# A two-layer language tower on one core: the expert stage with 71 blocks of 256 rows instead of 72

## The chip, the cores and the metric

The kernel runs on one core of one Trainium2 chip. The metric is the device time of the whole program in microseconds (us); lower is better. The program is one launch: every stage below runs once, one after the other, on the core's five engines (PE does the matmuls, DVE and ACT work on vectors, POOL gathers, scatters and computes a few small values, SP does nothing but issue DMAs) and its 16 DMA engines.

## The reference, cut to what matters

64 x 128 tokens with 192 features pass through an embedding with a layer norm, an attention layer, a mixture-of-experts layer, a second attention layer and a tree-shaped feed-forward layer. All of it is float32. The expert layer is the one that the change is about:

```
logits = xf @ Wr + br                       # xf: 8192 tokens x 192
gates = jax.nn.softmax(logits, axis=-1)
top_g, top_i = jax.lax.top_k(gates, K)      # K = 2 of E = 8 experts
for e in range(E):
    w_e = jnp.sum(top_g * (top_i == e), axis=-1)
    h = jax.nn.gelu(xf @ W1[e] + b1[e], approximate=False)   # 192 -> 768
    y = h @ W2[e] + b2[e]                                     # 768 -> 192
    out = out + w_e[:, None] * y
```

Each token counts for two experts alone, so 16384 rows have to be computed, in groups by expert.

## The kernel before, in words

The tokens are held in 64 tiles of 128 rows. The program has five stages.

**Layer 0** (embedding, first attention, router logits) is a software pipeline over the 64 tiles. `pipeline` (line 98) writes one step per tile on each engine; in step n a stage of age a works on tile n - a. It writes 12 steps out (for this layer), loops over the rest four steps at a time, and writes the steps that drain the pipeline out behind the loop. All engines have the same step order, and semaphores couple them. On SP (line 763), step n issues, in this order: two DMAs of 64 rows each that fill `posb`, the position rows of tile n (line 770); one DMA that writes zero rows from the tile `zrow` to a 64th of `xs_d` (line 773); and two DMAs of 64 rows that store the finished rows of tile n - 8 to `h1_d` (line 780). `posb` has two buffers, so the DMAs for tile n wait until DVE has read those of tile n - 2 (`emb_rd`). DVE reads `posb` and the gathered word rows `tok` in its `emb` step (line 635), one step after the load in the schedule. All of SP's DMAs stand on one queue, which the profile calls q1. POOL gathers `tok` on queue q0.

**Why zeros:** `xs_d` is the input of the expert stage in DRAM, `NBLK` blocks of 256 rows. The rows of an expert begin at a multiple of 256 and the blocks are not all full, so all rows are zeroed first. The view used at line 759 cuts `xs_d` into 64 pieces (one per tile), each of p partitions with `ZROWS` rows of 192 values behind each other. With 72 blocks there are 72 * 256 / 64 = 288 rows in a piece: 96 partitions of 3 rows.

**Routing** places each (token, choice) pair at a row of `xs_d`; then POOL scatters the normalised rows there (line 987), after it has waited for all 64 zero-fill DMAs (`xs_zero`, line 981). DVE also works out `etabi`, the expert of each block (lines 954 to 957); blocks behind the last group get expert 7 and hold zeros.

**The expert stage** is a pipeline over `NBLK` blocks with ages load 0, h 1, y 2. Each block loads its 256 rows, the weights of its expert (`w1h` and `w2h`, through a register that SP reads from `etabi`), splits the first weight into two parts on DVE, does 54 matmuls (line 1106 has 30 of them per block, line 1081 24), 6 gelu activations on ACT, and stores 256 rows to `ys_d`. `pipeline` writes 8 blocks out, loops over the other 64 in 16 rounds of 4, and drains with 2 steps.

**Layer 1** gathers the two expert rows of each token from `ys_d` and runs the second attention; **the last stage** does the tree-shaped layer and writes the output.

At the start of the program ACT too issues DMAs, on a queue of its own, q10 (lines 814 to 824): four loads of 21 rows (`wout`), four loads of 128 rows (`wqk`, `wv`, `wo`, `win`), three loads of 65 rows (`wqk`, `wv`, `wo`), one of 64 rows (`win`), and two stores to `rel_d` of 128 x 12 = 1536 rows each. ACT issues no other DMA in the whole program.

The functions that the change touches follow.

Of the kernel before, what the change touches and what calls it, by code (L numbers as in the profile page):

```python
# [15 lines left out]
T, B = 64, 128  # L16
# [6 lines left out]
E, TOPK, I = 8, 2, 768  # L23
NI = I // 128
BLK = 256
NBLK = T * B * TOPK // BLK + E
REL = 33
MAXREL = 16
LPAD = B - 1 - MAXREL
# [31 lines left out]
def upto(t, tiles=NT):  # L61

    return max(0, min(t + 1, tiles)) if isinstance(t, int) else t + 1


def after(eng, sem, value):

    if not isinstance(value, int) or value > 0:
        eng.wait_ge(sem, value)


UNROLL = 4
# [25 lines left out]
def pipeline(eng, ages, body, links=None, per=0, tiles=NT):  # L98


    head = UNROLL * (2 if max(ages.values()) < 8 else 3)

    for n in range(head):
        body(Step(ages, n, n // 2, n % UNROLL, tiles))
    at0 = links.at if links else 0
    with eng.Fori(0, (tiles - head) // UNROLL) as i:
        if links:
            links.base, links.at = at0 + i * (per * UNROLL), 0
        for p in range(UNROLL):
            body(Step(ages, UNROLL * i + (head + p), 2 * i + (head + p) // 2, p, tiles))  # L110
    if links:
        assert links.at == per * UNROLL, (links.at, per)
        links.base, links.at = 0, at0 + per * (tiles - head)
    for n in range(tiles, tiles + max(ages.values())):
        body(Step(ages, n, n // 2, n % UNROLL, tiles))


# [4 lines left out]
def settle(eng, spare):  # L122

    eng.sem_inc(spare, 1)


def tower(nc, ids_h, typ_h, tok_w, pos_w, type_w, gamma, beta,
          wqk0, wv0, wo0, w1h, b1h, w2h, b2h, wr, wqk1, wv1, wo1, relblk, rel32, win, wout, out):
    h1_d = nc.dram_tensor("h1_d", [T * B, D], F32).ap()
    xs_d = nc.dram_tensor("xs_d", [NBLK * BLK, D], F32).ap()  # L130
    ys_d = nc.dram_tensor("ys_d", [NBLK * BLK, D], F32).ap()
    route_d = nc.dram_tensor("route_d", [2 * TOPK, T * B], F32).ap()
    rel_d = [nc.dram_tensor(f"rel_d{p}", [B, ROWW], F32).ap() for p in range(2)]

    with ExitStack() as ctx:
        def sb(name, shape, dt=F32):
            return ctx.enter_context(nc.sbuf_tensor(name, shape, dt))
# [4 lines left out]
        def sem(name):  # L142
            return ctx.enter_context(nc.semaphore(name))
# [109 lines left out]
        small = sb("small", [128, 12, NT])  # L253
        etab = sb("etab", [128, NBLK])
        etabi = sb("etabi", [128, NBLK], I32)
        cnt = sb("cnt", [128, 6, E])
        cnti = sb("cnti", [128, E], I32)
        etmp = probT[0][:, 0:NBLK * E].rearrange("p (j e) -> p j e", e=E)
        wout4 = sb("wout4", [128, 4, D])


        def dsem(name):
            return sem("ld_" + name)

        const_ld = dsem("const")
        N_CONST = 14
        ZROWS = 3
        ids_ld = dsem("ids")
        late_ld = dsem("late")
        pool_c = sem("pool_c")  # L270
# [18 lines left out]
        def pool_steps(pool, l):  # L289
# [15 lines left out]
            def body(st):  # L305
# [16 lines left out]
                if st.has("z"):  # L322
                    rsqrt(st.tile("z"), st.two("z"), "mvz_ok", mvz, "rsz_ok", rsz, vepsz)
            pipeline(pool, ages, body, ch, 3 - l)

        def pe_transpose(pe, dst, src):
# [8 lines left out]
        def pe_steps(pe, l):  # L335
# [5 lines left out]
            def body(st):  # L341
# [166 lines left out]
                if st.has("z"):  # L508
                    pe.wait_ge(S["zn_ok"], done("z"))
                    pe_transpose(pe, ps_t[:, 256:512], zn[st.two("z")][:]).then_inc(S["zT_ps"], 1)  # L510
            pipeline(pe, ages, body)

        def act_steps(act, l):
# [5 lines left out]
            def body(st):  # L519
# [87 lines left out]
                if st.has("z"):  # L607
                    b = st.two("z")
                    act.wait_ge(S["zT_ps"], done("z"))
                    act.activation(zT0[b][:], ps_t[:, 256:384], ACT.Copy)  # L610
                    act.activation(zT1[b][0:D1, :], ps_t[0:D1, 384:512], ACT.Copy).then_inc(S["zT_sb"], 1)
            pipeline(act, ages, body)

        def dve_steps(dve, l):
# [131 lines left out]
        def _(sp):  # L746
# [11 lines left out]

            zr = xs_d.rearrange("(n p r) d -> n p (r d)", n=NT, r=ZROWS)
            sp.wait_ge(zero_ok, 2)  # L760
            h1_v = h1_d.rearrange("(t n c) d -> n c t d", n=NT, c=2)

            def body(st):
                if st.has("gather"):
# [4 lines left out]
                    for c in range(2):  # L769
                        sp.dma_start(posb[b][64 * c:64 * c + 64, :],  # L770
                                     pos_w[bass.ds(2 * t + c, 1), :].to_broadcast([64, D])).then_inc(M_["pos"][b], 16)

                    sp.dma_start(zr[bass.ds(t, 1)].rearrange("o p d -> (o p) d"), zrow[0:zr.shape[1], 0:ZROWS * D])\
                        .then_inc(xs_zero, 16)
# [90 lines left out]
        with nc.Block() as block:  # L865
# [9 lines left out]
            def _(pool):  # L875

                pool.iota(etabi[:], pattern=[[BLK, NBLK]], base=0, channel_multiplier=0).then_inc(B_["pool"], 1)
                pool.iota(cnti[:], pattern=[[-1, E]], base=E, channel_multiplier=0).then_inc(B_["pool"], 1)
# [118 lines left out]
        y_st = [sem(f"y_st{p}") for p in range(2)]  # L997
# [18 lines left out]
        with nc.Block() as block:  # L1016
            @block.sync
            def _(sp):
                hv = h1_d.rearrange("(t b) d -> b t d", b=B)

                def body(st):
                    before2 = upto(st.n - 2, NBLK)
                    if isinstance(st.n, int) and 4 <= st.n < 8:


                        c = st.n - 4
                        sp.dma_start(hres[:, 16 * c:16 * c + 16, :], hv[:, 16 * c:16 * c + 16, :])\
                            .then_inc(h1_ld[c], 16)
                    if st.has("load"):
                        t, b = st.tile("load"), st.two("load")  # L1030
                        ex = sp.value_load(etabi[0:1, bass.ds(t, 1)], min_val=0, max_val=E - 1)

                        after(sp, D_["h_sb"], NH * before2)
                        settle(sp, spare)
                        rows_ = xs_d[bass.ds(t * BLK, BLK), :].rearrange("(s p) d -> p s d", s=2)
                        sp.dma_start(xs[b][:, :, 0:D], rows_).then_inc(w1_ld[b], 16)
                        sp.dma_start(xs[b][:, :, D:XW], rows_[:, :, 128:D]).then_inc(w1_ld[b], 16)
                        loads = [(w1[b][0], w1h[bass.ds(ex, 1), 0:128, :]), (b1s[b][:], b1h[bass.ds(ex, 1)])]
                        loads += [(w1[b][1][r:r + D1, :], w1h[bass.ds(ex, 1), 128:, :]) for r in (0, D1)]
                        for dst, src in loads:  # L1040
                            sp.dma_start(dst, src.rearrange("o k i -> (o k) i")).then_inc(w1_ld[b], 16)

                        after(sp, D_["y_sb"], before2)
                        settle(sp, spare)
                        sp.dma_start(probT[b][:, 0:NI * D], w2h[bass.ds(ex, 1), :, :].rearrange("o k i -> (o k) i"))\
                            .then_inc(w2_ld[b], 16)
                        sp.dma_start(b2s[b], b2h[bass.ds(ex, 1), :].to_broadcast([128, D])).then_inc(w2_ld[b], 16)
                    if st.has("y"):
                        t, b = st.tile("y"), st.two("y")
                        sp.wait_ge(D_["y_sb"], upto(t, NBLK))  # L1050
                        settle(sp, spare)
                        sp.dma_start(ys_d[bass.ds(t * BLK, BLK), :].rearrange("(s p) d -> p s d", s=2), ys[b][:])\
                            .then_inc(y_st[b], 16)
                pipeline(sp, ages_d, body, tiles=NBLK)
                for p in range(2):
                    sp.wait_ge(y_st[p], 16 * (NBLK // 2))

            @block.tensor
            def _(pe):
# [335 lines left out]
def build(nc, arrays):  # L1395
    args = [nc.dram_tensor(n, x.shape, mybir.dt.from_np(x.dtype), kind="ExternalInput").ap()
            for n, x in arrays.items()]
    out = nc.dram_tensor("out_0_dram", [T, B, D], F32, kind="ExternalOutput").ap()
    tower(nc, *args, out)
# [11 lines left out]
```

## Time and profile before

| | |
|---|---|
| median of three runs | 2311.49 us (2299.59 to 2316.12) |
| the profiled execution's own time | 2312.43 us |
| its span, first to last instruction | 2310.7 us |
| PE busy | 1958.2 us, 85% of the span |
| DVE busy | 1397.8 us, 60% |
| ACT busy | 1011.0 us, 44% |
| POOL busy | 578.5 us, 25% |
| layer 0 | from 0 to about 640 us |
| routing and scatter | about 640 to 817 us |
| expert stage | 817 to about 1450 us |
| layer 1 | about 1450 to 2250 us |
| last stage | to 2310.7 us |

Busy shares are averages over stages of different kinds, so each stage is read by itself, with a table of stretches. A DMA issue in the profile ends when the descriptors are handed over, not when the data has landed; the time to landing stands with the issues. The share of a queue is the time that its packets took, summed over all packets, as a part of 16 DMA engines times the stretch. A packet is one contiguous row of a transfer, or one semaphore update of 4 bytes.

### The profile page before, as it was taken

Reading aid. Unit: us, or ns where it says so; the run is one execution under the profiler, and the core shown is the slowest. Engines: PE = TensorE matmul, PEld = TensorE weight load, DVE = VectorE, ACT = ScalarE, POOL = GpSimd, SP = SyncE. Lnnn points to the kernel's source line nnn. Section 1 sums busy time; section 2 is a strip of 40 time slices with the busy share of each in tenths; the row PEclk is TensorE's granted clock in tenths of the full one; section 3 lists DMA queues with packets and bytes.
Section 4 is the critical chain, followed back from the end, with each engine's and each line's share of the span. In section 5 each row is a group of like instructions: output and inputs, shape, how many; then the busy total and the mean of one; then the engine's idle time right before and its main releaser. Section 6 shows DMA issues by size and latency. Waiting matters only on the chain. (4 is left out here: it accounts for less than half of the span.)

```text
span 2310.7 us, 57088 instructions
## 1 busy us (share of the span) xinstructions
PE 1958.2 (85%) x18472; PEld 1776.6 (77%) x18472; DVE 1397.8 (60%) x3149; ACT 1011.0 (44%) x2767; POOL 578.5 (25%) x1167
## 2 busy tenths in 40 slices
PE   5999999999500058999999999699999999999985
PEld 4888888888400058999999999588888888888872
DVE  5777777776432224555555554477777777777735
ACT  2555555555200022333333333366666666666631
POOL 4343333432057700000000000433333333333100
PEclk8999999999655578999999999599999999999957
DMA  4122222221012279788888886465555555555513
GB/s 130 56 58 59 62 55 62 56 60 34 10 59 78 78 197 267 219 239 234 235 235 235 235 233 200 118 179 163 160 158 157 156 162 162 162 161 159 152 30 109
DMA packets 377119, 322.00 MB, mean 139 GB/s; under 512 B 55432, under 2 KB 337760, under 8 KB 377058
## 3 DMA queue, kind: packets, MB, share of 16 engines
q1 hardware_dynamic: 357592, 287.49, 43.8%
q0 software_dynamic: 15360, 31.48, 4.5%
q10 hardware_dynamic: 4106, 2.24, 0.4%
q8 instruction: 36, 0.59, 0.1%
q14 instruction: 25, 0.20, 0.0%
HBM read 209.51 MB, written 111.60 MB: 139 GB/s over the span
## 5 line engine op out<-in xcount | busy, mean ns | idle before, releaser
L1122 ACT ACTIVATE prob<-ps_s,b1s 128x256 f32<-128x256 f32 x432 | 181.3, 471 | 371.6 <-PE ps_s L1106 371.6
L1106 PE MATMUL ps_s<-xhi,w1hi_c 128*128 128x256 f32 x864 | 240.1, 296 | 2.6 <-DVE xhi L1144 2.6
L1106 PE MATMUL ps_s<-xhi,w1lo_c 128*128 128x256 f32 x864 | 230.3, 284 | 0.0
L1081 PE MATMUL ps_v<-probT,prob 128*128 128x192 f32 x864 | 214.8, 331 | 0.0
L1069 PE MATMUL ps_t<-ident,xs 128*128 128x128 f32 x144 | 38.8, 295 | 207.2 <-DMA score<-w1h 206.4
L1081 PE MATMUL ps_k<-probT,prob 128*128 128x192 f32 x864 | 214.0, 330 | 0.0
L1136 DVE CAST w1hi_c<-score 128x768 fp32r<-128x768 f32 x144 | 74.1, 557 | 225.3 <-DMA score<-w1h 225.3
L371 PE MATMUL ps_k<-xT,wqk_c 128*128 128x128 f32 (+1 forms) x1408 | 198.7, 291 | 0.6 <-ACT xT L606 0.6
L422 PEld LDWEIGHTS ps_v<-vv,probT 128*128 128x128 f32 x1536 | 189.1, 199 | 1.1 <-issue 1.0
L422 PE MATMUL ps_v<-vv,probT 128*128 128x17 f32 x1536 | 187.7, 262 | 0.5 <-DVE hres L674 0.5
L1069 PEld LDWEIGHTS ps_t<-ident,xs 128*128 128x128 f32 x144 | 20.7, 144 | 215.3 <-DMA score<-w1h 206.0
L371 PEld LDWEIGHTS ps_k<-xT,wqk_c 128*128 128x128 f32 (+1 forms) x1408 | 174.7, 198 | 10.1 <-ACT xT L606 1.0
L311 POOL COPY idx<-posi 128x1 uint32 (+1 forms) x64 | 11.6, 181 | 636.0 <-DVE posi L1212 636.0
L1106 PEld LDWEIGHTS ps_s<-xhi,w1hi_c 128*128 128x128 f32 x864 | 166.8, 193 | 3.0 <-issue 3.0
L371 PE MATMUL ps_q<-xT,wqk_c 128*128 128x128 f32 (+1 forms) x1152 | 167.4, 292 | 0.8 <-ACT xT L606 0.8
L1106 PEld LDWEIGHTS ps_s<-xhi,w1lo_c 128*128 128x128 f32 x864 | 167.0, 193 | 0.0
L355 PEld LDWEIGHTS ps_s<-kT,qT 32*64 32x64 f32 (+1 forms) x4608 | 111.8, 152 | 61.0 <-issue 60.8
L355 PE MATMUL ps_s<-kT,qT 32*64 32x64 f32 (+1 forms) x4608 | 154.3, 262 | 4.9 <-DVE score L730 3.8
L1081 PEld LDWEIGHTS ps_k<-probT,prob 128*128 128x128 f32 x864 | 155.0, 193 | 0.0
L1081 PEld LDWEIGHTS ps_v<-probT,prob 128*128 128x128 f32 x864 | 151.7, 194 | 0.0
L371 PEld LDWEIGHTS ps_q<-xT,wqk_c 128*128 128x128 f32 (+1 forms) x1152 | 145.8, 199 | 6.0 <-ACT xT L606 1.3
L547 ACT ACTIVATE prob<-score 128x768 f32<-128x768 f32 (+1 forms) x128 | 149.2, 1166 | 0.2 <-DVE score L730 0.2
(207 smaller groups left out, 4757.2 us busy)
## 6 DMA issues: line engine op xcount, KB each, us to landing
rel_d<-rpad SPq DMA_DIRECT2D x64, 864.0 KB, 4.4
relb<-rel_d SPq DMA_DIRECT2D x64, 768.0 KB, 5.1
probT<-w2h SPq DMA_DIRECT2D x72, 576.0 KB, 4.2
score<-w1h SPq DMA_DIRECT2D x72, 384.0 KB, 3.2
score<-w1h SPq DMA_DIRECT2D x144, 192.0 KB, 3.9
xs_d<-zrow SPq DMA_DIRECT2D x64, 216.0 KB
xs<-xs_d SPq DMA_DIRECT2D x72, 192.0 KB, 2.5
ys_d<-ys SPq DMA_DIRECT2D x72, 192.0 KB, 5.1
```

Of the source, the lines that this page charges most:

```text
L311: pool.tensor_copy(ix[b][:], ids_[:, bass.ds(t, 1)]).then_inc(S["idx_ok"], 1)
L355: last = pe.matmul(ps_s[t, g, a * keys:a * keys + keys], qT[q4][q, a // 2, t], kT[q4][q, a, t], start=True, stop=True)
L371: last = pe.matmul(bank[side][:, a * 128:a * 128 + 128], qk_w[l][chunk][:, o:o + 128], (xT0, xT1)[chunk][b][:, 0:128], start=(chunk == 0), ...
L422: last = pe.matmul(ps_v[:, j * W:(j + 1) * W], probT[b][:, j * 128:j * 128 + 128], vv[v][:, j * W:(j + 1) * W], start=True, stop=True)
L547: act.activation(prob[b][:, 0:H * keys].rearrange("p (g a k) -> p g a k", g=G, a=A), score[b][:, :, :, 0:keys], ACT.Exp, scale=SCALE).then ...
L1069: pe.transpose(ps_t[:, s * 128:s * 128 + 128], xs[b][:, s, 0:128], ident[:])
L1081: last = pe.matmul(ps_y[s][:, 0:D], hT[b][:, c, s * 128:s * 128 + 128], w2[b][:, c, :], start=(c == 0), stop=(c == NI - 1))
L1106: last = pe.matmul(dst, w, x, start=(k == 0), stop=(k == len(terms) - 1))
L1122: last = act.activation(hT[b][:, c, :], ps_s[:, j, (c % 2) * BLK:(c % 2) * BLK + BLK], ACT.Gelu, bias=b1s[b][:, c:c + 1])
L1136: ch.step(dve.tensor_copy(w1hi[b][c][:], w1[b][c]))
```

## The change

There are at most 71 blocks that can hold rows: eight experts' row counts, each rounded up to 256, with a sum of 16384 before rounding. The change sets `NBLK` to 71. Two things follow in the code.

First, 71 - 8 = 63 is not a multiple of 4. `pipeline` now loops 15 rounds of 4 and writes the last three blocks out behind the loop, ahead of the two draining steps. The pipelines of the layers have 64 tiles and stay as they are. The final wait of SP counts 36 stores for one buffer and 35 for the other.

Second, `xs_d` has 71 * 256 = 18176 rows, and each of the 64 pieces that layer 0 zeroes has 284. That isn't a multiple of 3, so `ZROWS` is 4: a piece is 71 partitions of 4 rows.

```diff
-NBLK = T * B * TOPK // BLK + E
+NBLK = T * B * TOPK // BLK + E - 1
@@ def pipeline
-    with eng.Fori(0, (tiles - head) // UNROLL) as i:
+    rounds = (tiles - head) // UNROLL
+    with eng.Fori(0, rounds) as i:
         if links:
             links.base, links.at = at0 + i * (per * UNROLL), 0
         for p in range(UNROLL):
             body(Step(ages, UNROLL * i + (head + p), 2 * i + (head + p) // 2, p, tiles))
     if links:
         assert links.at == per * UNROLL, (links.at, per)
-        links.base, links.at = 0, at0 + per * (tiles - head)
-    for n in range(tiles, tiles + max(ages.values())):
+        links.base, links.at = 0, at0 + per * UNROLL * rounds
+    for n in range(head + UNROLL * rounds, tiles + max(ages.values())):
         body(Step(ages, n, n // 2, n % UNROLL, tiles))
@@ def tower
-        ZROWS = 3
+        ZROWS = 4
@@
                 for p in range(2):
-                    sp.wait_ge(y_st[p], 16 * (NBLK // 2))
+                    sp.wait_ge(y_st[p], 16 * ((NBLK + 1 - p) // 2))
```

Line numbers behind line 105 are one higher in the changed kernel. Below are instructions of SP in their order, with the shape that a DMA writes. The first place is a step of layer 0 just ahead of the loop. Before (`xs_d<-zrow` is the zero fill, `h_d<-hres` the store to `h1_d`):

```order
L770 DMA posb<-pos_w 64x192 x2
L773 DMA xs_d<-zrow 96x576
L780 DMA h_d<-hres 64x192 x2
L106 UNCONDITIONAL_BRANCH
```

and changed:

```order
L771 DMA posb<-pos_w 64x192 x2
L774 DMA xs_d<-zrow 71x768
L781 DMA h_d<-hres 64x192 x2
L107 UNCONDITIONAL_BRANCH
```

Nothing has moved, but the zero fill writes 71 rows of 768 values where it wrote 96 rows of 576. It does so in all 64 steps.

The second place is SP's last block in the expert stage's loop and what stands behind the loop. Before:

```order
L1047 DMA tok<-b2h 128x192
L1052 DMA ys_d<-ys 128x2x192
L106 REGISTER_ALU
L106 COMPARE_AND_BRANCH
L1052 DMA ys_d<-ys 128x2x192 x2
L1016 UNCONDITIONAL_BRANCH
```

and changed, the first of three such blocks:

```order
L107 REGISTER_ALU
L107 COMPARE_AND_BRANCH
L1032 TENSOR_LOAD etabi
L1032 ISA x2
L1037 DMA xs<-xs_d 128x2x192
L1038 DMA xs<-xs_d 128x2x64
L1042 ISA
L1042 DMA score<-w1h 128x768
L1042 ISA
L1042 DMA b1s<-b1h 128x6
L1042 ISA
L1042 DMA score<-w1h 64x768 x2
```

Three blocks stand behind the loop's branch and the loop has one round less, on this engine as on PE, ACT and DVE.

## Rows read from the trace of the kernel before

**Rows 1.** The page: span, and busy time (share of the span) with the instructions.

```profile
span 2310.7 us, 57088 instructions
PE 1958.2 (85%) x18472; PEld 1776.6 (77%) x18472; DVE 1397.8 (60%) x3149; ACT 1011.0 (44%) x2767; POOL 578.5 (25%) x1167
```

**Rows 2.** Stretches: length, busy time by engine, PE's granted clock, DMA share, GB/s.

```profile
93.00:550.00 457.00, 451.59 (x6270) 388.44 (x6268) 345.76 (x1043) 256.94 (x939) 172.24 (x415) 1.00 0.22 59
550.00:640.00 90.00, 60.39 (x672) 47.92 (x658) 45.58 (x127) 29.58 (x109) 9.13 (x26) 0.75 0.05 10
910.00:1380.00 470.00, 456.32 (x3279) 450.49 (x3278) 240.25 (x454) 171.60 (x395) 0.00 (x0) 1.00 0.81 233
1380.00:1450.00 70.00, 63.03 (x455) 62.13 (x454) 30.83 (x65) 23.88 (x55) 0.42 (x3) 0.99 0.66 189
```

**Rows 3.** Zero fill, `posb` load and its reader: duration, first and last start; landing.

```profile
L773 SPq DMA_DIRECT2D xs_d<-zrow x64: 324/437/1747, 9.4 to 540.6; - x64
L773 SPq FUSED_REGOPS  x52: 42/43/43, 92.7 to 540.5; - x52
L770 SPq DMA_DIRECT2D posb<-pos_w x128: 465/529/1256, 8.1 to 539.9; - x128
L635 DVE TENSOR_TENSOR emb<-tok,posb x64: 348/353/359, 15.1 to 550.8; 128x192 f32<-128x192 f32 x64
DMA to landing us min/median/max: 2.4/2.7/8.0
```

**Rows 4.** Waits from 93 to 550 us (engine, line, releaser: us, times, longest).

```profile
POOL veps L298 <- DVE mvb L662: 226.0, 52, 4.9
...
DVE emb L635 <- issue: 0.2, 1, 0.2
```

**Rows 5.** DMA from 93 to 550 us: packets by size, queues, issues.

```profile
DMA packets 24944, 26.93 MB, mean 59 GB/s; under 512 B 4989, under 2 KB 19113, under 8 KB 24937
...
q1 hardware_dynamic: 22441, 21.73, 18.1%
q0 software_dynamic: 2496, 5.12, 3.7%
...
xs_d<-zrow SPq DMA_DIRECT2D x52, 216.0 KB
h_d<-hres SPq DMA_DIRECT2D x104, 48.0 KB
posb<-pos_w SPq DMA_DIRECT2D x102, 48.0 KB, 2.6
tok<-tok_w,idx POOLq DMA_INDIRECT x52, 3.4
```

**Rows 6.** The page: queue q10, which ACT alone uses (packets, MB, share).

```profile
q10 hardware_dynamic: 4106, 2.24, 0.4%
```

**Rows 7.** DMA from 1209.0 to 1209.5 and from 1208.8 to 1209.8 us: q1.

```profile
q1 hardware_dynamic: 46, 0.21, 102.3%
...
q1 hardware_dynamic: 101, 0.40, 98.9%
```

**Rows 8.** Loads of expert rows (L1036): all of them, then from 910 us.

```profile
L1036 SPq DMA_DIRECT2D xs<-xs_d x72: 378/385/5662, 817.2 to 1425.8; - x72
L1036 SPq DMA_DIRECT2D xs<-xs_d x63: 378/385/398, 910.6 to 1425.8; - x63
```

**Rows 9.** Waits from 910 to 1380 us, the expert loop.

```profile
ACT prob L1122 <- PE ps_s L1106: 285.6, 169, 5.7
DVE w1hi_c L1136 <- DMA score<-w1h: 150.7, 55, 4.8
```

**Rows 10.** POOL's scatter (L987): duration, first and last start.

```profile
L987 POOL DMA_INDIRECT xs_d<-xn,sidx x64: 956/959/1065, 651.2 to 806.7; - x64
```

## The prediction

> **What bounds the kernel now.** I read the page first: PE is busy for 85% of a 2310.7 us span, no other engine for more than 60% [rows 1]. That is an average, so next the stretches. From 93 to 550 us, the steady part of layer 0, PE is busy 451.59 of 457 us at the full granted clock, while the DMA engines are busy 22% of the time [rows 2]: PE sets the pace, DMA is idle four fifths of it. In the expert loop, 910 to 1380 us, PE is busy 456.32 of 470 us and the DMA engines 81%. PE sets that pace too, with loads close behind it: DVE waits for weights 55 times, 150.7 us in all, ACT waits for PE [rows 9]. So a block taken out of the expert stage is worth a block's period. But the change also alters a DMA in every step of layer 0, and there the question is not how busy DMA is on average but how the work is spread over the 16 engines.
>
> **One block less.** SP issues the loads of 63 blocks between 910.6 and 1425.8 us [rows 8]: 515.2 / 62 = 8.31 us per block. The stage is a chain of blocks with nothing beside it, so all of it comes off the end: -8.3 us. It drains as before.
>
> **Three blocks behind the loop.** The same instructions, but fetched once instead of being repeated. The nearest rows are the eight blocks written out ahead of the loop: their loads go from 817.2 to 902 us, or from the first row of all to the first of the 63: (910.6 - 817.2) / 9 = 10.4 us per block [rows 8], 2.1 us over the loop's. That includes filling the pipeline and reloading `hres`, 6 MB, beside it, so it is an upper end: 3 x 2.1 = +6 us. The lower end is 0: just behind the loop, in the drain, PE is still busy 63.03 of 70 us [rows 2]. I take +0.5. The loop's trip count, the chain counts and the final waits (36 and 35 stores) cost nothing: they are constants in waits that stand there anyway.
>
> **The zero fill on 71 partitions.** The bytes hardly change (96 x 2304 = 221 kB per tile, now 71 x 3072 = 218 kB). What changes is the number of rows, and the trace shows that a DMA's rows are not always dealt to all 16 engines. Queue q10 carries ACT's 14 DMAs and nothing else, 4106 packets [rows 6]. Its data rows are 4 x 21 + 4 x 128 + 3 x 65 + 64 + 2 x 1536 = 3927. The other 179 are semaphore updates. That each engine taking part writes one such update is seen in layer 0: packets under 512 B, 4989 from 93 to 550 us, are 16 for each of the 310 DMAs issued there (4960) and a few at the edges [rows 5]. Were it always 16, q10 would have 14 x 16 = 224. The seven DMAs whose row count divides by 16 give 112. The other seven have to give 67: 13 for each of the three with 65 rows and 7 for each of the four with 21 rows make 39 + 28 = 67 exactly. 13 and 7 are the largest divisors of 65 and 21 up to 16. 96 rows went to 16 engines, 6 each. 71 is prime: by the same rule, all 71 rows go to one engine.
>
> What that engine then has to do for each tile, from rows:
> - Its zero rows. Where nearly only large packets were in flight, 0.21 MB took 102.3% of 16 x 0.5 us (8.2 us of engine time) and 0.40 MB took 98.9% of 16 x 1 us (15.8) [rows 7]: 25.6 and 25.3 kB per us. 218 kB take 8.5 to 8.6 us; I take 8.5.
> - Its sixteenth of everything else: two `posb` loads, two stores, the gather. Each is 48 or 96 kB, 295 kB in all, 18.4 kB for one engine, 0.73 us at 25.3 kB per us: the lower end. The upper end is what the trace has: q1 and q0 took 21.8% of 457 us over 52 tiles, 1.92 us per engine and tile [rows 5], less 0.55 for the old zero fill: 1.37 us, with all the crowding of 16 engines that start at once. I take 0.9, nearer the lower end, since fifteen of the sixteen no longer move zeros.
>
> That makes 9.4 us per tile (9.2 to 9.9), against a period of (540.6 - 92.7) / 51 = 8.78 us [rows 3]. PE's work for a tile, 451.59 / 52 = 8.7 us, fits into 9.4. So **one DMA engine becomes the bound of layer 0**, with fifteen nearly idle.
>
> How it comes to the path: `posb` of tile n stands on queue q1 behind the zero fill of tile n - 1, and its share on the crowded engine goes in order. DVE's `emb` waits for it, and with it `emb_rd`, `emb`'s followers, PE. Today the slack is large: the last `posb` is issued at 539.9 us, lands 2.7 us later and is read at 550.8 [rows 3]; in the steady part `emb` never waits for a DMA, its one wait of 0.2 us is for issue [rows 4]. That slack of 8.2 us is used up once. The engine is never idle, since SP issues the next tile's DMAs as soon as DVE has read two tiles back, while a whole zero fill is still to run. The first fill is issued at 9.4 us [rows 3]. Of the 2.4 us that a `posb` needs at the least to land [rows 3], I put some 1.5 before its rows move or after them, at either end. So the last `posb` lands at 11 + 63 x 9.4 - 2 (eight early tiles have no store) + 1.5 = 603 us, and DVE reads it there instead of at 550.8: **+52 us**. This is from the start of the program, since before it ran ahead in the early steps, which the queue doesn't allow now. The drain behind it (PE 60.39 of 90 us) is as long as before. The last zero fill ends some 9 us later, at 612, and the scatter comes a whole routing stage after the drain (651.2 - 550.8 = 100 us after the last `emb` today [rows 3, 10]), so it waits for nothing new.
>
> Of this rows can't show one thing: whether successive one-engine transfers use the same engine. If they took turns, each would have 8.6 us of zeros in 16 tiles. I take the same one; the other is a rival below. The Trainium skill, "DMA: Bandwidth & Descriptors", section "Why a DMA increments its semaphore by 16 and not by 1", says both: the count is the largest k up to 16 that divides the slowest dimension on both sides, and SP's and ACT's DMAs use the lowest-numbered k. With the first the trace agrees (179 updates on q10); the second no run here shows yet. That sentence is why the rival gets so little.
>
> **Sum.** 2312.4 (the profiled execution, 0.9 above the median) + 52 - 8.3 + 0.5 = 2356.6; against the median 2355.7. I forecast **2356 us**, 1.9% slower. Case ends: 9.2 us per tile gives +39 and in all 2343 (less the 0.9: 2342); 9.9 gives 52 + 63 x 0.5 = +83, and with +6 for the cold blocks 2392.
>
> **Rivals.**
> - *The other side: the zero fill stays harmless and only the block counts.* Either 71 rows are spread unevenly over 16 engines, or successive fills take turns. An engine then has at most 8.6 us of zeros once in a while, and the slack of 8.2 us [rows 3] covers it: `emb` doesn't wait. 2311.5 - 8 = 2303 us, no change by the measure. It decides at the point where the most loaded engine needs less than 8.78 us per tile. For it: no transfer of the trace has a prime count of rows. Against it: the exact count of 179 updates. Chance 0.09.
> - *One engine, but it keeps pace.* Alone it might be faster than 25.6 kB per us; it needs (8.78 - 0.9) us or less for 218 kB, 27.7 kB per us. Then only the early steps cost, which now run ahead: tile 12 was zeroed at 92.7 us [rows 3], 12 x 8.7 + 11 = 115, 22 us later, less 8.2 of slack: +14 - 8 = 2318 us. Against it: no large stretch is above 25.9. Chance 0.04.
> - *One engine, and far slower.* q1 as a whole moved 21.73 MB in 18.1% of 16 x 457 us, 16.4 kB per us [rows 5]. 218 kB at that take 13.3 us, 14.2 with the rest: 11 + 63 x 14.2 = 906, +355 - 8 = 2659 us. For it: a row of stores into one DRAM area from one engine is nowhere in the trace. Against it: that average has small packets and crowding in it. A milder form is that PE, idle 0.7 of 9.4 us per tile, loses its clock; against that, at 63.03 of 70 us busy it kept 0.99 [rows 2]. Chance 0.05.
> - *Faster by over 1%*: no row offers more than one block. 0.01.
>
> The forecast's case has 0.81. A measurement of this kernel tells a difference of about 1% from none: below 2288 faster, above 2335 slower. All of the main case and the slow rival lie above: slower 0.86; the harmless ones between: same 0.13; faster 0.01. The range: the main case from 2342 to 2392, with what is outside it at 0.19; its upper end holds little, and below it the milder mixtures (turns taken in part, less crowding) lie closer: 2338 to 2390.
>
> **What would show each step.** In the profile after: the zero fill's semaphore packets, one instead of 16 for each, so q1 has 64 x 15 = 960 fewer of them, 64 x 25 = 1600 fewer data rows, and less one block's; `emb` (now L636) waiting for `posb` in most tiles of layer 0, and `posb` landing some 9 us after its issue instead of 2.7; a spacing of zero-fill issues of 9.4 us; PE busy some 92% of the steady part; the last `emb` near 603 us; the expert stage one 8.3 us period shorter with no gap behind the loop; layer 1 and the last stage the same in length. Wrong I would be if `posb` still lands in 3 us (the rule of divisors doesn't hold here, or turns are taken), or if the tiles come at 8.8 us with `posb` late (the engine's rate), or if the last three blocks take more than 10 us each.

## The result, and the profile after

The changed kernel takes 2348 us against 2313 us before (medians): the ratio is 1.0146, 95% interval 1.0115 to 1.0178, so **34 us slower** (27 to 41). One block less was worth about 8 us, so the change cost about 42 us elsewhere. Two of its seven executions took 2706 and 2708 us, with TensorE's granted clock at 1.2 GHz through nearly all of layer 0; the ratio is made without them (the other five took 2342 to 2349 us), but the profiled execution is one of them, and its layer 0 has to be read with that in mind.

The page of that execution, span, busy time, granted clock and packets:

```profile
span 2706.5 us, 56836 instructions
PE 2342.1 (87%) x18414; PEld 2112.1 (78%) x18414; DVE 1397.5 (52%) x3141; ACT 1014.1 (37%) x2760; POOL 578.2 (21%) x1167
PEclk9755555555555555557999999996999999999977
DMA packets 373009, 319.89 MB, mean 118 GB/s; under 512 B 53944, under 2 KB 335632, under 8 KB 372946
```

The last row holds the evidence for the main mechanism. There are 4110 packets fewer than the 377119 of before, of them 1488 under 512 B (55432 before). A block accounts for 1408 data rows and 9 x 16 = 144 semaphore updates; of its data rows 384 are under 512 B. That is 528 of the 1488. The other 960 are 64 fills times 15 updates: each fill now posts one update, not 16. The rest fits too: 64 x 25 = 1600 fewer zero rows, 1552 + 960 + 1600 = 4112, and two more packets of instruction fetch. By the count of updates, all 71 rows went to one engine.

What that did to the first tiles, before the clock fell at 97.1 us: first queue q1 and SP's issues between 20 and 90 us (last number: median us to landing), then waits between 20 and 97 us (us, times, longest):

```profile
q1 hardware_dynamic: 1760, 2.34, 9.8%
...
xs_d<-zrow SPq DMA_DIRECT2D x8, 213.0 KB
posb<-pos_w SPq DMA_DIRECT2D x15, 48.0 KB, 10.7
```

```profile
DVE emb L636 <- DMA posb<-pos_w: 37.2, 8, 6.9
...
PE ps_t L328 <- DVE xn L683: 33.5, 3, 28.4
```

`posb` lands 10.7 us after its issue where it took 2.7 [rows 3], DVE's `emb` waits for it in each of the 8 tiles, and PE waits for what follows from `emb`. SP itself is held as well, as its timeline shows (start, us, engine, line):

```profile
24.84 7.25 SPq L771 DMA_DIRECT2D posb<-pos_w  x2
32.14 0.61 SPq L774 DMA_DIRECT2D xs_d<-zrow  x1
34.70 8.38 SPq L771 DMA_DIRECT2D posb<-pos_w  x2
43.13 0.44 SPq L774 DMA_DIRECT2D xs_d<-zrow  x1
```

Two `posb` issues together take 7 to 8 us, where the kernel before took 1.10 us for them in the same stretch. That is about the pace of the crowded engine, as if SP could not hand over more while the fills ahead were unfinished; the trace shows the time, not the reason.

From 100 to 900 us the stretches are another matter:

```profile
100.00:900.00 800.00, 800.00 (x6247) 695.11 (x6247) 351.35 (x1048) 262.60 (x938) 173.31 (x418) 0.50 0.13 34
```

At half clock PE is busy all the time and tiles come 15.4 us apart, so the crowded engine is hidden again. The expert stage, loads of rows (all blocks; from the ninth on; the last three):

```profile
L1037 SPq DMA_DIRECT2D xs<-xs_d x71: 378/388/4262, 1226.3 to 1820.9; - x71
L1037 SPq DMA_DIRECT2D xs<-xs_d x63: 378/387/395, 1308.4 to 1820.9; - x63
L1037 SPq DMA_DIRECT2D xs<-xs_d x3: 390/390/394, 1805.1 to 1820.9; - x3
```

(1820.9 - 1308.4) / 62 = 8.27 us per block against 8.31 [rows 8], and the last three, which stand behind the loop, were loaded 7.9 us apart.

### The profile page after: what moved, and what is told of

Its sections match the earlier page's. It is cut to its first block and busy times, and to the rows that moved or that the text cites. A ratio compares the mean times of both kernels' runs of the same rounds, so it can differ in the third digit from the quotient of the medians.

```text
span 2706.5 us, 56836 instructions
## 1 busy us (share of the span) xinstructions
PE 2342.1 (87%) x18414; PEld 2112.1 (78%) x18414; DVE 1397.5 (52%) x3141; ACT 1014.1 (37%) x2760; POOL 578.2 (21%) x1167
## 5 line engine op out<-in xcount | busy, mean ns | idle before, releaser
L372 PE MATMUL ps_k<-xT,wqk_c 128*128 128x128 f32 (+1 forms) x1408 | 275.6, 366 | 0.6 <-ACT xT L607 0.6
L372 PEld LDWEIGHTS ps_k<-xT,wqk_c 128*128 128x128 f32 (+1 forms) x1408 | 245.5, 267 | 13.0 <-ACT xT L607 1.0
L675 DVE TENSOR_TENSOR hres<-ps_v,hres 128x192 f32 (+1 forms) x128 | 45.7, 357 | 365.8 <-PE ps_v L334 365.8
L372 PE MATMUL ps_q<-xT,wqk_c 128*128 128x128 f32 (+1 forms) x1152 | 220.5, 354 | 1.3 <-ACT xT L607 1.3
L356 PEld LDWEIGHTS ps_s<-kT,qT 32*64 32x64 f32 (+1 forms) x4608 | 134.4, 200 | 90.7 <-issue 90.5
L372 PEld LDWEIGHTS ps_q<-xT,wqk_c 128*128 128x128 f32 (+1 forms) x1152 | 195.2, 256 | 6.4 <-ACT xT L607 1.7
L356 PE MATMUL ps_s<-kT,qT 32*64 32x64 f32 (+1 forms) x4608 | 183.0, 319 | 11.7 <-DVE score L731 11.2
L333 PE MATMUL ps_v<-wv_c,xT 128*128 128x192 f32 x384 | 155.5, 501 | 0.1
```

The lines of the kernel that those rows point to most:

```text
L333: pe.matmul(dst, x0, w[0][:], start=True, stop=False)
L356: last = pe.matmul(ps_s[t, g, a * keys:a * keys + keys], qT[q4][q, a // 2, t], kT[q4][q, a, t], start=True, stop=True)
L372: last = pe.matmul(bank[side][:, a * 128:a * 128 + 128], qk_w[l][chunk][:, o:o + 128], (xT0, xT1)[chunk][b][:, 0:128], start=(chunk == 0), ...
L675: dve.tensor_tensor(h, ps_v[:, 0:D], h, ALU.add).then_inc(S["y_ok"], 1)
```

## The experiments

Each kernel was timed beside the kernel before on its chip. In the first three groups that kernel took 2352 to 2357 us, in the last 2308, so ratios are compared, and microseconds only within a group. In the slower cases layer 0 runs at 9.1 to 9.4 us per tile (9.3 to 9.4 with an even fill) instead of 8.78; this matters below.

| kernel | rows per fill on the loaded engine | ratio to before | 95% interval | us | before |
|---|---|---|---|---|---|
| the change again | 71, all tiles | 1.0059 | 1.0032 to 1.0086 | 2363 | 2352 |
| even fill, 71 blocks | 4 | 0.9977 | 0.9958 to 0.9997 | 2344 | 2352 |
| 72 blocks, 71-row fill | 71, all tiles | 1.0093 | 1.0060 to 1.0127 | 2369 | 2352 |
| fill issued by ACT | 71, all tiles | 1.0048 | 1.0028 to 1.0067 | 2362 | 2352 |
| 59 + 12 rows | 60, all tiles | 0.9989 | 0.9957 to 1.0021 | 2351 | 2357 |
| 62 rows | 31 on each of two | 0.9964 | 0.9933 to 0.9995 | 2349 | 2357 |
| 71 rows in the loop | 4, then 71 | 0.9917 | 0.9899 to 0.9935 | 2340 | 2357 |
| 89 rows in the loop | 4 longer ones, then 89 | 1.1226 | 1.1194 to 1.1259 | 2650 | 2357 |
| 79 rows in the loop | 4 longer ones, then 79 | 1.1124 | 1.1089 to 1.1158 | 2614 | 2353 |
| 71 rows in the head | 71, then 4 | 1.0052 | 1.0023 to 1.0080 | 2368 | 2353 |
| even fill again | 4 | 0.9968 | 0.9953 to 0.9983 | 2345 | 2353 |
| 71 rows in the loop, again | 4, then 71 | 0.9997 | 0.9975 to 1.0018 | 2308 | 2308 |

### Which part of the change costs

The change unedited:

> The changed kernel once more, for a profile at the full granted clock. Theory A (one DMA engine carries all 71 zero rows and bounds layer 0): about 2346 us; zero-fill issues 9.1 to 9.4 us apart in the loop instead of 8.78; DVE's emb waits for posb in most tiles; the last emb near 590 us instead of 550.8; expert stage one period of 8.3 us shorter. Rival B (the three blocks behind the loop cost the time): layer 0 as long as before, the last three blocks over 20 us each. Rival C (something else in the stages behind layer 0): tiles 8.78 us apart, and a later stage longer by 40 us.

It came out 11 us above the kernel before, not 34, in a group with slower tiles. No full-clock profile of it was had: the profiled execution ran layer 0 at 1.2 GHz again (2722 us).

The zeros in another shape, the same 54528 values per tile:

```diff
-            zr = xs_d.rearrange("(n p r) d -> n p (r d)", n=NT, r=ZROWS)
+            zr = xs_d.rearrange("(n q) d -> n (q d)", n=NT).rearrange("n (p c) -> n p c", p=64)
@@
-                    sp.dma_start(zr[...], zrow[0:zr.shape[1], 0:ZROWS * D])
+                    sp.dma_start(zr[...], zrow[0:64, 0:zr.shape[2]])
```

> 71 blocks, but each tile's zeros are written as 64 partitions of 852 values instead of 71 of 768: the same 54528 values, 4 rows for each of 16 engines. Theory A: the whole loss is the shape of the zero fill, so 2313 - 8 = 2305 us, tiles 8.78 us apart, posb landing in 2.7 us, no wait of emb for it. Rivals B and C: still about 2346 us.

Measured 2344 us, 8 below the kernel before and 19 below the change beside it. From 93 to 550 us `emb` waits for no DMA, and its tiles are (541.4 - 99.6) / 47 = 9.40 us apart:

```profile
L636 DVE TENSOR_TENSOR emb<-tok,posb x48: 350/354/359, 99.6 to 541.4; 128x192 f32<-128x192 f32 x48
```

The whole loss is the shape of the fill. Run again in the third group it gave 0.9968, 8 us below before: this version beats both kernels. It was not timed in a group with tiles 8.78 us apart.

> The even fill (64 rows of 852 values) once more beside the two kernels above: 8 us under the kernel before, tiles as far apart as before.

The opposite, 72 blocks with the 71-row fill:

```diff
-        ZROWS = 3
+        ZROWS = 4
@@
-            zr = xs_d.rearrange("(n p r) d -> n p (r d)", n=NT, r=ZROWS)
+            zr = xs_d[0:71 * BLK, :].rearrange("(n p r) d -> n p (r d)", n=NT, r=ZROWS)
+            sp.dma_start(xs_d[71 * BLK:72 * BLK, :].rearrange("(p r) d -> p (r d)", p=128), zrow[:, 0:2 * D]).then_inc(xs_zero, 16)
@@
-                pool.wait_ge(xs_zero, 16 * NT)
+                pool.wait_ge(xs_zero, 16 * (NT + 1))
```

> 72 blocks as before, with the zero fill alone changed: 71 partitions of 768 values per tile, and one DMA of 128 partitions more at the start for the last block's rows. Theory A: 2313 + 42 = 2355 us, the change's time plus one block. Rivals B and C: 2313 us.

2369 us: 17 above before, 6 above the change, where one block makes 8. The mechanism is there without the other edits. The expected size, 42, was that of the first comparison. Here the engine needs less than the 9.4 us of a tile, and only the early tiles are lost, as the kernels with the fills split between head and loop show below. Rivals B and C (a cost behind the loop or in a later stage) are out.

### How the rows are dealt

Two engines, and one with fewer rows:

```diff
+            zr = xs_p.rearrange("o (n p c) -> (o n) p c", n=NT, p=62)     # xs_d with room behind it
+                    sp.dma_start(zr[...], zrow[0:62, 0:880])
```

> 71 blocks; the zeros of a tile as 62 rows of 880 values (62 = 2 x 31, so two engines if divisors decide, 31 rows of 3520 bytes each, 4.2 us). Theory A: hidden, 8 us under the kernel before. Rival E (only counts that divide by 16 are spread, everything else goes to one engine): 62 rows at 0.135 us are 8.4 us on one engine: as slow as the change.

```diff
+                    for lo, hi in ((0, 59), (59, 71)):
+                        sp.dma_start(zr[...][lo:hi, :], zrow[lo:hi, 0:ZROWS * D]).then_inc(xs_zero, 16)
@@
-                pool.wait_ge(xs_zero, 16 * NT)
+                pool.wait_ge(xs_zero, 32 * NT)
```

> 71 blocks; the 71 zero rows of a tile go in two DMAs, 59 rows (prime: one engine) and 12 rows (one to each of 12). The loaded engine has 60 rows instead of 71: 7.1 us of zeros and some 0.6 to 0.8 of the rest, 7.8 us per tile, below the period of layer 0. Theory A (throughput of one engine): hidden in the loop, a few us lost at most in the first tiles: 7 to 0 us under the kernel before. Rival D (latency: posb has to wait for the fill ahead of it, whatever the total): most of the change's loss stays, 10 to 40 us over the kernel before.

Each page counts the packets under 512 B. The even fill's, that of 62 rows, and that of 59 + 12:

```profile
DMA packets 373521, 319.89 MB, mean 137 GB/s; under 512 B 54904, under 2 KB 336592, under 8 KB 373458
```

```profile
DMA packets 372497, 319.89 MB, mean 136 GB/s; under 512 B 54008, under 2 KB 335696, under 8 KB 372434
```

```profile
DMA packets 373777, 319.89 MB, mean 136 GB/s; under 512 B 54712, under 2 KB 336400, under 8 KB 373714
```

The even fill posts 16 updates. 62 rows post 896 = 64 x 14 fewer, so 2 per fill; 59 + 12 rows post 192 = 64 x 3 fewer, so 13, which is 1 + 12; and the change's 71 rows post 960 = 64 x 15 fewer. 1, 1, 2, 12 and 16 are the largest divisors up to 16 of 71, 59, 62, 12 and 64. Both kernels keep the block's gain within their intervals (8 and 6 us by the medians). With 60 rows on one engine, `emb` still waits six times, all in the first 146 us:

```profile
L636 DVE TENSOR_TENSOR emb<-tok,posb x16: 348/354/359, 14.8 to 146.8; 128x192 f32<-128x192 f32 x16
...
  DMA posb<-pos_w: 24.9, 6
```

So a late `posb` by itself costs something only in the early tiles; in the loop a loss needs more work on one engine than the period holds. Rivals D and E are out, D by these waits more than by the time: the twelfth `emb` came at 110.0 us against 93.9 with 62 rows, and the loop won most of that back, with tiles 9.1 us apart against 9.4. Why it was quicker is not shown; the last section comes back to it.

### Early tiles and steady part

The fills of the 12 written-out steps even, those of the loop on one engine:

```diff
+                    if isinstance(t, int):                                # the 12 written-out steps
+                        sp.dma_start(ze[...], zrow[0:64, 0:852]).then_inc(xs_zero, 16)
+                    else:
+                        sp.dma_start(zr[...], zrow[0:71, 0:768]).then_inc(xs_zero, 16)
```

> 71 blocks; the 12 written-out steps of layer 0 zero their tiles with 64 rows of 852 values over 16 engines, the 52 steps of the loop with 71 rows on one engine. It splits the change's loss into the early tiles and the steady part. Theory A: the steady part loses 52 x (9.2 - period) less the slack of 8 us: with a period of 8.78 us +14 and with the block 5 over the kernel before, with a period of 9.4 us nothing and 8 under it. Theory F (the steady part carries all of the loss): 35 over the kernel before at 8.78 us, 10 over at 9.4.

and the reverse (`if not isinstance(t, int)`):

> 71 blocks; the reverse of the kernel with one engine in the loop: 71-row fills in the 12 written-out steps, even fills of 64 rows in the loop. Theory A: this has all of the change's loss where the period is 9.4 us, since only the early tiles are held to 9.0 us each: +19 over the even fill, 11 over the kernel before. The clock: if it is the early starvation that costs TensorE its clock, the profiled execution falls to half clock near 97 us and takes about 2720 us, as the change's does; if it is the steady part, it doesn't.

With a period of 9.4 us the head has all of the loss: 1.0052, as the change's 1.0059; its executions at full clock have a median of 2364 us, 19 over the even fill beside it. Its profiled execution kept the full clock, so it shows what the profile after can't: the first 12 tiles of `emb` in it, and in the kernel before.

```profile
L636 DVE TENSOR_TENSOR emb<-tok,posb x12: 357/359/359, 14.9 to 117.6; 128x192 f32<-128x192 f32 x12
...
  DMA posb<-pos_w: 39.6, 11
```

```profile
L635 DVE TENSOR_TENSOR emb<-tok,posb x12: 349/354/359, 15.1 to 94.8; 128x192 f32<-128x192 f32 x12
```

The twelfth tile comes 22.8 us later (24.0 against the even fill of the same group, 93.6 us). The expectation on the clock was not settled: the profiled execution kept it, but one of the four executions took 2726 us. So early starvation alone can cost it, and doesn't always. The two profiles show how near the two cases are. The stretch ahead of 97.1 us in the changed kernel, where the clock then fell, and in this one, where it didn't (length, then PE, PEld, DVE, ACT, POOL, clock, DMA share, GB/s):

```profile
94.00:97.10 3.10, 2.30 (x31) 1.54 (x31) 2.21 (x6) 1.02 (x5) 2.09 (x7) 1.00 0.07 28
```

```profile
94.00:97.10 3.10, 2.30 (x31) 1.52 (x31) 2.20 (x6) 1.04 (x6) 2.09 (x6) 1.00 0.07 28
```

Of the 26 executions of kernels in which SP issues 71-row fills in the head, five lost the clock so (2706 to 2730 us); of the 45 with even, 62 or 59 + 12 rows there and at most 71 in the loop, none did.

The loop's fills alone gave more than expected, 0.9917, which is 17 us below before instead of 8. That wasn't understood, so it was run again.

> The kernel with one-engine fills in the loop alone, once more: it came out 17 us under the kernel before where one block alone explains 8. If that is real, 0.992 of the kernel before again; if it was the spread of the runs, 0.9965 as the even fill. On a chip whose tiles come 8.78 us apart it should be 1.002 to 1.006 instead.

This time the kernel before took 2308 us beside it, and there it is 0.9997: the block's gain of 8 us is used up again, as expected of a steady part that loses 52 x (9.15 - 8.78) = 19 less the slack of 8. Whether the 17 us are real where the tiles are slower, this doesn't settle. The queue's pace is visible in SP's timeline and in the waits from 120 to 540 us:

```profile
411.13 0.29 SPq L779 DMA_DIRECT2D xs_d<-zrow  x1
415.33 3.16 SPq L786 DMA_DIRECT2D h_d<-hres  x2
418.76 1.24 SPq L772 DMA_DIRECT2D posb<-pos_w  x2
420.19 0.29 SPq L779 DMA_DIRECT2D xs_d<-zrow  x1
...
447.73 0.28 SPq L779 DMA_DIRECT2D xs_d<-zrow  x1
```

```profile
DVE emb L636 <- DMA posb<-pos_w: 13.1, 23, 0.7
```

(447.73 - 411.13) / 4 = **9.15 us per tile**, with `emb` waiting a little in half of the tiles, and two stores that take SP 3 us to issue. In the `emb` starts the tiles come 8.78 us apart from the 13th to the 33rd (98.4 to 274.0 us) and 9.15 from there to the 57th (493.7), so the slack lasted for about 20 tiles, 20 x 0.37 = 7.4 us. From the 13th `emb` to the last it took 459.4 us against 447.1 before: 12 us lost. The wait rows total 13.1 us; that each is so short suggests that engines, queue and SP had fallen into step.

### The engine's rate, and the clock

More rows than a tile has time for, in the loop alone (`xs_d` has room behind it for the rows written beyond a piece):

```diff
+                        sp.dma_start(zr[...], zrow[0:89, 0:768])          # or 79
```

> As the kernel with the even fill in the written-out steps, but the loop's fills are 89 rows of 768 values (prime; 18 rows of each are written twice, over zeros of the next piece, with room behind xs_d). One engine: 89 x 0.118 = 10.5 us of zeros, 11.2 us per tile with the rest. Theory A: tiles 11.2 us apart at full clock, emb waiting for posb in nearly every one, 52 x (11.2 - period) - 8 - 8: +109 over the kernel before with a period of 8.78, +78 with 9.4. Rival G (the engine is not the bound, fills run beside other work): no more than the change.

> As the kernel with 89 rows in the loop, but 79 rows (prime): 9.3 us of zeros, 9.9 to 10.0 us per tile with the rest. Theory A with the clock: if TensorE's granted clock holds, tiles come 9.9 us apart, emb waits for posb, and layer 0 is 52 x (9.95 - 9.4) - 8 = 20 us longer than with the even fill (50 on a chip with 8.78). Theory H (any wait in the steady part of some 6% costs the clock): it falls to half as with 89 rows, tiles 15.4 us apart, and the time is near 2650 us.

Both began as theory A has it. Fills while the clock was full, with 79 rows and with 89:

```profile
165.63 0.42 SPq L780 DMA_DIRECT2D xs_p<-zrow  x1
...
205.97 0.28 SPq L780 DMA_DIRECT2D xs_p<-zrow  x1
```

```profile
132.28 0.29 SPq L780 DMA_DIRECT2D xs_p<-zrow  x1
143.38 0.28 SPq L780 DMA_DIRECT2D xs_p<-zrow  x1
154.69 0.28 SPq L780 DMA_DIRECT2D xs_p<-zrow  x1
```

(205.97 - 165.63) / 4 = 10.1 us and 11.2 us. With 9.15 for 71 rows that is 0.11 to 0.12 us for each further row of 3072 bytes: rival G is out, and so is the idea that successive fills take turns among engines, since then no fill of this size could set a pace. Then, at about 213 and 160 us, the granted clock fell to 1.2 GHz and stayed there to the end of the layer. Stretches of the kernel with 79 rows, then of that with 89:

```profile
160.00:200.00 40.00, 38.65 (x537) 33.09 (x535) 29.11 (x87) 20.98 (x79) 15.02 (x38) 1.00 0.18 54
200.00:240.00 40.00, 38.44 (x373) 33.10 (x369) 21.40 (x64) 15.47 (x56) 11.69 (x27) 0.67 0.17 53
240.00:400.00 160.00, 160.00 (x1255) 138.80 (x1254) 71.06 (x214) 52.87 (x189) 33.45 (x81) 0.50 0.12 35
```

```profile
120.00:160.00 40.00, 36.19 (x512) 30.60 (x512) 27.05 (x83) 20.62 (x79) 13.96 (x33) 1.00 0.17 52
180.00:700.00 520.00, 520.00 (x4072) 451.64 (x4072) 226.92 (x677) 170.44 (x608) 112.95 (x271) 0.50 0.13 38
```

A mean over 40 us hides what PE did just ahead of the fall. With 79 rows it waited 0.59 us until 211.34 and 0.64 us until 212.42, and the clock fell at about 213.4; with 89 rows it waited 1.11 us in one piece until 156.43, 0.46 and 0.64 us behind it, and the clock fell at about 160.1:

```profile
210.00:212.00 2.00, 1.19 (x16) 0.61 (x14) 1.09 (x4) 0.62 (x3) 1.11 (x3) 1.00 0.06 26
```

```profile
155.00:157.00 2.00, 0.89 (x16) 0.64 (x15) 1.78 (x6) 0.87 (x2) 1.04 (x4) 1.00 0.16 58
```

Theory H, put up after the 89 rows, was right for the 79 (2614 us, where it said near 2650): the 79 rows are 261 us over the kernel before, the 89 rows 292, where the even fill is 8 under it. At 15.4 us per tile instead of 10.1 or 11.2, nearly all of it is clock and hardly any of it DMA.

### The queue or the engine

```diff
-                    sp.dma_start(zr[...], zrow[...]).then_inc(xs_zero, 16)          # SP, line 774
+                if l == 0 and st.has("gather"):                                     # ACT, first thing in its step
+                    act.dma_start(zr[...], zrow[...]).then_inc(xs_zero, 16)
```

> 71 blocks, the 71-row zero fill issued by ACT on its own queue (q10) instead of SP's (q1), one per step. The one engine has the same bytes. Theory A1 (posb suffers because it stands behind the fill on the same queue): posb gets its turn within a row or two, the fill falls some 0.4 us per tile behind and ends before the scatter asks for it at 650 us: about 2305 us, plus what ACT's 64 issues cost it, at most a few us. Theory A2 (the engine as a whole is the bound, whatever the queue): 2346 us again.

2362 us, as the change. But the trace is not that of A2. From 93 us on `emb` waits for `posb` not once, and its tiles are (597.0 - 95.8) / 55 = 9.1 us apart:

```profile
L640 DVE TENSOR_TENSOR emb<-tok,posb x56: 350/354/359, 95.8 to 597.0; 128x192 f32<-128x192 f32 x56
...
  issue: 0.2, 1
```

The loss came ahead of that, from ACT itself. Its first activation waited for the issues in front of it, until 42.1 us; in the kernel before that was 20.2 us:

```profile
ACT L608 <- issue: 42.1, 1, 42.1
```

```profile
19.74 22.37 ACTq L523 DMA_DIRECT2D xs_d<-zrow  x4
```

Four fills took ACT 22.37 us to issue, and each of the next three 7.0 to 8.1 us, the stall that SP had in the changed kernel. (The two `rel_d` stores of 1536 rows stand ahead of them on the queue; how much of the first wait is theirs was not separated.) So another queue takes the fill out of `posb`'s way, and an engine that computes is the wrong one to issue it. Whether it would help at 8.78 us per tile was not tried.

## Why the prediction was right, and what it had too large

- **The rule of divisors** was read off 179 semaphore updates on q10 [rows 6], and holds for 71, 59, 62, 12 and 64 rows. The Trainium skill, "DMA: Bandwidth & Descriptors", section "Why a DMA increments its semaphore by 16 and not by 1", states it; the packet counts agree exactly.
- **The same engine each time.** No row of the trace before shows this; it rested on the Trainium skill, which says it in the same section (the lowest-numbered k). The fills set a pace of 9.15, 10.1 and 11.2 us, which they could not if they took turns. So the harmless rival failed at its second leg too.
- **The rival "one engine, but it keeps pace"** has what happened in the groups with slower tiles, though not for its reason: the engine was no faster, the period was longer. It put the early loss at 22 us less the slack; measured were 22.8 and 24.0 us at the twelfth tile and 19 us in all.
- **One engine becomes the bound of layer 0**: right, +42 us against +52 forecast. The mis-sized term is the engine's load for a tile, 9.4 us forecast, 9.15 measured. The two pieces were 8.5 for the zeros and 0.9 for the rest; 0.11 to 0.12 us per row makes 7.8 to 8.5 of the first, so the measurements don't divide the 0.25 us between them. Over 63 tiles it is 16 us, more than the 10 by which the forecast was too high. Split in two, the loss adds up: the early tiles 22.8 us, measured in the head alone, and the loop 52 x (9.15 - 8.78) = 19 us, worked out from the pace, 42 in all. The changed kernel itself was never profiled at full clock, so its last `emb` (603 us forecast) and its spacing of fills were not seen.
- **The slack of 8.2 us is used up once**: seen where the loop's fills alone are on one engine. There the tiles come 8.8 us apart for 20 tiles (7.4 us of slack) and 9.15 later, and the total is 0.9997.
- **One block, -8.3 us**: the even fill gave -5 and -8 us by its ratios, and the period is 8.27 us in the profile after.
- **The blocks behind the loop cost 0 to 6 us**: they cost nothing, 7.9 us apart.
- **The clock.** The forecast gave it half a sentence and the argument that 63.03 of 70 us busy kept 0.99 [rows 2]. That was wrong as an argument: with 79 rows it fell at 213 us though PE was busy 38.65 of the 40 us from 160 to 200; two waits of 0.59 and 0.64 us came just ahead of it. Had the engine needed one microsecond more per tile, the forecast would have been some 250 us too low. It came out in the range because 9.15 us is near enough to what PE needs, and with some luck: five executions of seven kept the clock, and the ratio is made of those.

## What to carry to other kernels

Before a tile shape is changed, look at the row count of every DMA that follows from it: 96 rows of 2304 bytes and 71 rows of 3072 are the same bytes, but 16 engines against one. A share of 22% for the DMA engines says nothing of one engine, while the count of small packets in the profile tells at once how many engines each transfer had. And a wait that seems to cost a few tenths of a microsecond per tile can cost TensorE its clock, so time it with a little more of the same wait before it is trusted.

## What the runs showed that was not expected

- **The granted clock fell and did not come back.** Once at 1.2 GHz, PE was busy 800 of 800 us in the changed kernel and the clock stayed at 0.50 until the layer ended; tiles took 15.4 us instead of about 9. In the kernel before it fell too, at 32 us, and was back at 1.00 by 52.5 us:

```profile
32.00:52.00 20.00, 19.80 (x169) 17.73 (x168) 14.51 (x39) 6.54 (x23) 9.35 (x20) 0.50 0.24 70
```

  The Trainium skill, "TensorE: Matmul & The Clock Gate", section "Part 1: The HAM clock gate (the "warmup" mystery)", says that activity releases the throttle. The kernel before agrees; in the changed one a busy share of 100% did not do it. What decides was not found, neither for the fall nor for the return. A mean busy share over a long stretch does not: the even fill held 1.00 at 423.86 of 457 us, with single waits of PE up to 0.9 us, and the 79-row kernel lost it at 38.65 of 40.
- **SP stalls at issue when one engine is behind.** Two `posb` issues took 7 to 8 us with 71 rows per fill, two stores 3.0 to 3.2 us in the steady part, against about 1.1 to 1.3 us. ACT had the same stall when it issued the fills.
- **The same layer at 8.78 or 9.4 us per tile**: the kernel before took 2308 to 2313 us or 2352 to 2357. It is not the chip alone: the first group (2352) and the last (2308) are on record with the same chip number. In the slower case PE waits for DVE's `on` (24.0 us from 120 to 540 us in the even fill) where it didn't before. Three kernels wait less for it: 17.0 us with 71 rows in the loop, 10.3 with 59 + 12, 6.5 with ACT's fills, and their tiles come 9.2, 9.1 and 9.1 us apart. So the 9 us that the loop fills gained over the even fill may be a better phase between the engines, but no run tested that, and why the layer has two periods stays open.
